# Softmax denominators summed by ScalarE over the maxima's tiles, and values multiplied as they leave their bank

## The reference

```python
q = x @ Wq.T + bq; k = x @ Wk.T + bk; v = x @ Wv.T + bv      # 16 query heads, 4 key heads, 32 wide
q = _apply_rope(q); k = _apply_rope(k)
att = jnp.einsum('bhgqd,bhkd->bhgqk', q, k) / scale
att = jnp.where(causal, att, jnp.asarray(-jnp.inf, att.dtype))
att = jax.nn.softmax(att, axis=-1)
y = jnp.einsum('bhgqk,bhkd->bhgqd', att, v)
return y @ Wo.T + bo
```

## Time and profile before

| | |
|---|---|
| median of 3 runs | 2018.44 us (2017.76 to 2019.21) |
| the profiled execution | 2016.81 us, span 2015.1 us |
| TensorE / VectorE / ScalarE / GpSimd busy | 83% / 44% / 28% / 23% of the span |
| granted TensorE clock, mean | 0.888 of full |
| start until the first score exponential | 110.3 us |
| the attention's last values copied out (L1066) | 1067.9 us |

### The profile page before, as it was taken

How to read it: one execution, slowest core, us unless ns; L and a number is a source line. 1 busy time by engine, 2 the same in 40 slices (tenths; PEclk the granted TensorE clock), 3 DMA queues, 4 the chain that set the end, 5 groups by cost and what they waited for, 6 DMA issues and landing times.

```text
span 2015.1 us, 23148 instructions
## 1 busy us (share of the span) xinstructions
PE 1669.5 (83%) x7518; PEld 1002.2 (50%) x7519; DVE 882.4 (44%) x1986; ACT 570.8 (28%) x1083; POOL 467.3 (23%) x653
## 2 busy tenths in 40 slices
PE   4488888888888888888865599999799999999940
PEld 4254554555545555455433487888444444444420
DVE  2444547456464564645634453222222222222239
ACT  2133324234342343423442211111122222222213
POOL 0111222122221222212211112222122222222237
PEclk8678888888898888988976799999899999999975
DMA  3344354254542545415332336775457664665468
GB/s 121 47 78 75 79 126 106 73 130 92 126 111 74 126 95 126 116 43 126 80 136 73 152 130 223 244 260 177 154 135 239 163 190 103 162 163 129 74 183 348
DMA packets 117598, 271.53 MB, mean 135 GB/s; under 512 B 15364, under 2 KB 40966, under 8 KB 110600
## 3 DMA queue, kind: packets, MB, share of 16 engines
q1 hardware_dynamic: 100984, 232.42, 39.9%
q0 software_dynamic: 16496, 37.63, 9.5%
HBM read 248.62 MB, written 109.34 MB: 178 GB/s over the span
## 4 chain that ended last, share of the span: by engine, by line
PE 66%; DVE 11%; issue 8%; ACT 5%; DMA 4%; POOL 4%; SPq 1%; POOLq 0%; DVEq 0%; ACTq 0%
PE bank L1767 26%; PE bank L1968 11%; PE bank L1985 5%; PE bank L1871 4%; PE bank L1848 4%; PE bank L1874 3%; PE bank L1831 3%; DVE tmp L1230 2%; PE bank L1958 1%; PE bank L1972 1%; ACT P L1058 1%; DVE rp L1238 1%; PE bank L1833 1%; ACT xin L1016 1%; PE bank L1978 1%
## 5 line engine op out<-in xcount | busy, mean ns | idle before, releaser
L1298 DVE TENSOR_REDUCE mx<-bank 128x1 f32<-128x512 f32 (+3 forms) x352 | 219.3, 634 | 209.4 <-PE bank L1833 208.4
L1058 ACT ACTIVATE P<-bank 128x512 f32<-128x512 f32 x320 | 190.5, 595 | 411.2 <-PE bank L1848 410.4
L1968 PE MATMUL bank<-ring,xg 128*128 x632 | 285.1, 594 | 0.0
L1831 PE MATMUL bank<-Ks,Qs 96*128 96x384 f32 (+3 forms) x512 | 167.4, 394 | 68.3 <-DVE mx L1298 36.7
L1848 PE MATMUL bank<-Qs,Ks 97*128 97x512 f32 x320 | 162.1, 507 | 42.9 <-ACT P L1058 37.1
L1767 PE MATMUL bank<-xt,ws 128*128 128x512 f32 x768 | 182.9, 395 | 2.7 <-DMA xt<-xt_scratch 2.7
L1968 PEld LDWEIGHTS bank<-ring,xg 128*128 128x128 f32 x632 | 114.3, 191 | 114.6 <-issue 114.6
L1767 PEld LDWEIGHTS bank<-xt,ws 128*128 128x128 f32 x768 | 146.2, 190 | 35.7 <-DMA xt<-xt_scratch 3.6
L1674 POOL TENSOR_SCALAR_AFFINE_SELECT P<-P 128x256 f32<-128x256 f32 (+1 forms) x192 | 93.2, 488 | 301.8 <-ACT P L1058 301.7
L1831 PEld LDWEIGHTS bank<-Ks,Qs 96*128 96x128 f32 x512 | 107.9, 228 | 109.7 <-DVE mx L1298 51.8
L1767 PE MATMUL bank<-wo_s,ynr 128*128 128x512 f32 x384 | 132.0, 470 | 35.0 <-DVE x L1357 23.9
(11 more groups left out here) (227 smaller groups left out, 2396.9 us busy)
## 6 DMA issues: line engine op xcount, KB each, us to landing
ring<-in_w SPq DMA_DIRECT2D x79, 1024.0 KB
ring<-in_w SPq DMA_DIRECT2D x79, 512.0 KB
Qs<-st SPq DMA_DIRECT2D x192, 128.0 KB, 4.7
xs<-xs_scratch SPq DMA_DIRECT2D x79, 258.0 KB, 3.7
xs_scratch<-xs_scratch SPq DMA_DIRECT2D x78, 258.0 KB, 5.0
xt<-xt_scratch SPq DMA_DIRECT2D x32, 512.0 KB, 6.4
xs<-xn_scratch SPq DMA_DIRECT2D x64, 256.0 KB, 2.9
xt_scratch<-xt SPq DMA_DIRECT2D x30, 512.0 KB, 4.8
```

What stands on the lines that cost most here:

```text
L1058: e.activation(Pt[:, p, :], bank[PA.bank[step]][:, :], ACT.Exp, scale=SCALE).then_inc(s_exp, 1)
L1298: e.tensor_reduce(mx[:, G % 2, :].rearrange("p (h i) -> p h i", i=4)[:, h:h + n, i:i + 1], bank[PA.bank["max", b, p, j]][:, 0:n * k].rearr ...
L1831: e.matmul(ps[:, o * k:o * k + k], Qs[0:96, 4 * g + h + o, i * 128:(i + 1) * 128], Ks[0:96, b % 2, g, 0:k], start=o == 0, stop=False)
L1968: e.matmul(ps[:, :].rearrange("p (o n) -> p o n", o=1), xg[:, q, 128 * k:128 * k + 128], ring[:, bass.ds(reg[n], 1), 512 * k:512 * k + 512 ...
```

## The change

Denominators no longer come from TensorE. After VectorE has reduced a first-pass tile (now to minima, since the scores are formed with the opposite sign), ScalarE takes the exponential of the same tile in place, with the row's minimum as bias pointer and the sum along the row as a second output: one instruction for each head, 512 in all. VectorE takes reciprocals of 128x16; minima and reciprocals are turned together (32 columns for 16), both split in two, and go out in four DMAs: two rows (96 and 97) of Qs and two rows of a small tile rd. `rb` spreads the reciprocals with one product per quarter of a batch, before the last `pv` of it; ScalarE copies the spread ones to SBUF, VectorE multiplies the values as they leave their bank, and the product is split from there. The ones-matmuls, the denominators' bank and their chain at the end of a batch go. Maxima get the freed third bank, `maxT` moves to the general ones, and the rates change.

```diff
-    G, M, U, PS = Banks(0, 3), Banks(3, 2), Banks(5, 1), Banks(0, NP)
+    G, M, U, PS = Banks(0, 3), Banks(3, 3), Banks(6, 1), Banks(0, NP)
...
+        def tiles():
+            for n in range(NMAX + 2):
+                if n < NMAX:
+                    P.on(M, P.add("max", b, p, n))
+                if 1 <= n <= NMAX:
+                    P.add("mred", b, p, n - 1)
+                if n >= 2:
+                    P.add("mexp", b, p, n - 2)
+                    M.done(P.bank["max", b, p, n - 2])
                 yield
-            s = P.add("maxT", b, g)
-            P.on(M, s)
-            yield
-            P.add("mTcp", b, g)
-            M.done(P.bank[s])
-        for n in range(NMAX):
-            s = P.add("max", b, p, n)
-            P.on(M, s)
-            if n > 0:
-                M.done(P.bank["max", b, p, n - 1])
-            yield
-            if n == 5:
-                yield from wait(4)
-            if n == MAX_OF[0] + 1:
-                P.add("maxdo", b, p, n)
-                M.done(P.bank["max", b, p, n])
+                if n == 5:
+                    yield from wait(4)
+        def turns():
+            for j in range(2):
+                g = 2 * p + j
+                while ("mexp", b, p, MAX_OF[j] - 1) not in P.nth:
+                    yield
                 yield
-                yield from turn(2 * p)
-        P.add("maxdo", b, p, NMAX - 1)
-        M.done(P.bank["max", b, p, NMAX - 1])
-        yield
-        yield from turn(2 * p + 1)
-        yield
+                P.add("mrec", b, g)
+                yield
+                yield from claim("maxT", b, g)
+                yield
+                P.add("mThi", b, g)
+                yield
+                P.add("mTlo", b, g)
+                freed("maxT", b, g)
+                yield
+        yield from beside(tiles(), turns())
...
+                after.extend([("rbs", b, p, qh), ("ymul", b, p, qh), ("yhi", b, p, qh), ("ylo", b, p, qh)])
...
+                    if late[0] < qh:
+                        yield from claim("rb", b, p, late[0])
...
-        side = [(maxima(b, 1), 1.3)]
+        side = [(maxima(b, 1), 1.35)]
         if more:
-            side.append((chain(prep(b + 1), proj(b + 1, 0), move(b + 1, 0, 0)), 46 / H))
+            side.append((chain(prep(b + 1), proj(b + 1, 0), move(b + 1, 0, 0)), 2.0))
             nought = zeros(b)
             side.append((islice(nought, 6), 0.25))
         if tails is not None:
-            side.append((islice(tails, 34), 34 / H))
+            side.append((islice(tails, 24), 24 / H))
...
+            side.append((maxima(b + 1, 0), 1.35))
...
+            side.append((tails, 1.3))
...
+                    for n in range(2):
+                        e.dma_start(Qs[96 + n:97 + n, 4 * g:4 * g + 4, :].bitcast(F32), mT[0:16, G % 2, n, :].bitcast(F32)).then_inc(
+                            d_m[G % 2], 16)
+                    for n in range(2):
+                        r = 4 * n + 2 * (g % 2)
+                        e.dma_start(rd[r:r + 2, g // 2, :, :].bitcast(F32), mT[16:32, G % 2, n, :].bitcast(F32)).then_inc(d_m[G % 2], 16)
...
+                elif kind == "mexp":
+                    b, p, j = a
+                    g_, h, n, i = MAX_TILES[j]
+                    G, k = 4 * b + 2 * p + g_, 128 * (i + 1)
+                    ps = bank[PA.bank["max", b, p, j]]
+                    w.wait_ge(max_dve, PA.nth["mred", b, p, j])
+                    if G >= 2:
+                        w.wait_ge(l_dve, G - 1)
+                    for o in range(n):
+                        c = 4 * (h + o) + i
+                        m = e.activation(ps[:, o * k:o * k + k], ps[:, o * k:o * k + k], ACT.Exp, scale=-1.0, bias=mr[:, G % 2, 0, c:c + 1],
+                                         accum_out=se[:, G % 2, c:c + 1])
+                    m.then_inc(max_act, 1)
...
+                    e.activation(reciprocals_of(b, p, qh), bank[PA.bank["rb", b, p, qh]][:, :], ACT.Copy).then_inc(rbs_act, 1)
+                elif kind == "yhi":
+                    b, p, qh = a
+                    w.wait_ge(y_dve, PA.nth["ymul", b, p, qh])
+                    e.activation(values_of(b, qh)[:, 0, 2 * p:2 * p + 2, :],
+                                 bank[PA.bank["rb", b, p, qh]][:, :].rearrange("p (h q) -> p h q", h=2), ACT.Copy).then_inc(y_hi, 1)
...
+                elif kind == "mrec":
+                    b, g = a
+                    G = 4 * b + g
+                    w.wait_ge(max_act, PA.nth["mexp", b, g // 2, MAX_OF[g % 2] - 1])
+                    e.reciprocal(mr[:, G % 2, 1, :], se[:, G % 2, :]).then_inc(l_dve, 1)
...
+                    e.tensor_tensor(ps[:, :], bank[7][:, :], reciprocals_of(b, p, qh), ALU.mult).then_inc(y_dve, 1)
...
+                    e.tensor_tensor(y[:, 1, 2 * p:2 * p + 2, :], bank[PA.bank["rb", b, p, qh]][:, :].rearrange("p (h q) -> p h q", h=2),
+                                    y[:, 0, 2 * p:2 * p + 2, :], ALU.subtract).then_inc(y_lo, 1)
...
-                        e.matmul(queries(bank[6][32 * j:32 * j + 32, :], qh, kc), Vs[:, b % 2, kc, 2 * p + j // 2, :], rows[j],
-                                 start=kc == 0, stop=last)
-                    for j in range(4):
-                        m = e.matmul(queries(bank[7][32 * j:32 * j + 32, :], qh, kc), ov[:, n, :], rows[j],
-                                     start=kc == 0 and n == 0, stop=last and n == 3)
+                        m = e.matmul(queries(bank[7][32 * j:32 * j + 32, :], qh, kc), Vs[:, b % 2, kc, 2 * p + j // 2, :], rows[j],
+                                     start=kc == 0, stop=last)
...
-                        m = e.matmul(ps[:, :], sel_s[:, 2 * p + qh, :], rc[:, n, :], start=n == 0, stop=n == 1)
-                    m.then_inc(rb_pe, 1)
+                    e.matmul(bank[PA.bank[step]][:, :].rearrange("p (h q) -> p h q", h=2), sel_s[:, :], rd[:, p, :, 256 * qh:256 * qh + 256],
+                             start=True, stop=True).then_inc(rb_pe, 1)
```

More of the change, by code:

```diff
@@ L253, in values, with turn @@
             if kc == 2 * qh + 1:
-                P.add("yev", b, p, qh)
+                after.extend([("rbs", b, p, qh), ("ymul", b, p, qh), ("yhi", b, p, qh), ("ylo", b, p, qh)])
+        def turn():
+            if after:
+                s = P.add(*after.pop(0))
+                if s[0] == "ylo":
+                    freed("rb", *s[1:])
         for qh in range(2):
@@ L268, in heads @@
                 late = (qh, kc, slots)
+        yield from claim("rb", b, p, 1)
         values(*late)
-        yield
-    def values_ready(b, qh):
-        for p in range(3):
-            if p < 2:
-                yield from claim("rb", b, qh, p)
-            if p > 0:
-                P.add("ynm", b, qh, p - 1)
-                freed("rb", b, qh, p - 1)
-            yield
-            if p > 0:
-                P.add("ynhi", b, qh, p - 1)
-                yield
-                P.add("ynlo", b, qh, p - 1)
-                yield
+        while after:
+            yield
+            turn()
     def front(b, i):
@@ L339, in tail @@
             yield from beside(back(b, 0), front(b, 1))
-            yield from beside(back(b, 1), chain(values_ready(b, 1), front(b, 2)))
+            yield from beside(back(b, 1), front(b, 2))
             yield from beside(back(b, 2), front(b, 3))
@@ L352, in rest @@
     def rest():
-        for j in range(5):
+        for j in range(4):
             P.add("late", j)
@@ L1663, in _ @@
                     e.tensor_tensor(st[o, 2:4, :], rp[o, :, :], st[o, 0:2, :], ALU.subtract).then_inc(st_lo, 1)
-                elif kind == "late" and a[0] == 4:
+                elif kind == "late" and a[0] == 3:
                     e.memset(zero[:, :], 0.0).then_inc(pool_const, 1)
```

243 lines of the change are left out of this document (91 added, 152 removed).

## The result

The changed kernel takes 2313.45 us (median of 4, 2312.28 to 2316.18), the kernel before on the same chip 2018.15 (4 runs). The ratio is 1.146, 95% interval 1.144 to 1.148: 295 us slower. I had forecast slower by 37. Direction and stalls were right, the size was not.

The account below looks back on a forecast made before the run. PE was taken to bound the batch, busy 85%. Batches 1 to 6 +55, batch 0 -3, batch 7 -8, end -11, start +4: +37 on 2018.4 gave 2055 us, forecast range 2022 to 2095 (0.48), 8 in 10 between 1975 and 2125.

Parts of the forecast that it names:

- The wait for Q: Middle of batches 1 to 6: PE stands 17 us (14 to 20) at the first maxima tile for Q's DMA.
- ScalarE's price: New exponentials with sums cost ScalarE 17 us per half batch (14 to 20), the sums 2.9 of it, ceiling 5.7.
- stretch 1: First 16 scores of batch 3's first half: ACT, busy 33 us, ends it at 38 us for 50.3.
- PE's relief: Ones-matmuls and half the spreading go from PE's path: 11.3 us per batch, 90 in eight batches.
- The spreading matmul: L1885, from two products per half to one: 1.3 of 2.7 us per batch go, 1.2 expected to show.
- over 80%: Sign of a right forecast: ACT's busy share in stretch 1, at about 33 us.
- Stretches 2 and 3: First half's last four scores: 43 us (26 plus a 17 us stall) for 19.9; second half: 54.4 for 56.0.
- Batch 0: First batch, 101.7 us, without a stall: PE -11, ACT nearly as long as PE, so -3 us.
- Rival (c): Granted clock falls from 0.88 to 0.80 over the whole attention: 2115 us, chance 0.03.
- Rival (b): ACT saturates, output-tile steps wait behind exponentials and PE for them: about 2125 us, chance 0.12.
- The end: Behind the last batch, output products start earlier without the denominators' chain: -11 us.
- The start: Kernel start, where extra DMA issues and the first tiles' longer chain are not hidden: +4 us.

Follow-up runs that it names:

- run 3: Changed kernel, with the planner freeing a transposed input tile's bank before the next transpose claims one: 2163.3 us median, 2117 fastest.
- run 9: Kernel before, with the ones-matmuls kept only for the first block of keys of each group: 2003.2 us, ratio 0.993.
- run 4: Changed kernel with the bank freed first as in run 3 and all 512 new exponentials left out as in run 2: 1975.5 us, ratio 0.979.
- run 6: Changed kernel with 80 idle products on PE in each of the six waits for Q: 2288.5 us, ratio 1.134.
- run 12: Kernel before, with 512 exponentials and sums added on ScalarE whose results nobody uses: 2156.7 us, ratio 1.069.
- run 2: Changed kernel without the 512 new exponentials, a tile's bank free after VectorE's minimum: 2130.3 us, ratio 1.057.
- run 8: Kernel before, with each of the 320 score products done twice: 2054.5 us, ratio 1.017.
- run 15: run 3 with statistics and normalization of the input planned earlier, at the end of the batch ahead: 2119.8 us, ratio 1.050.
- run 1: Changed kernel without the sums along the row, denominators a constant: 2264.7 us, ratio 1.123.
- run 14: run 3 with two banks instead of three for the maxima, one score bank and one bank idle: 2503.5 us, ratio 1.242.

## Why the prediction was right and wrong

- **The wait for Q** held: 16.5 to 17.4 us six times, forecast 17 (14 to 20). K's products end at 666.16 and the tile starts at 695.00: 28.8 for 28.9. Without it (run 3) the time is 150 to 196 us less, not 103.
- **ScalarE's price** held: 17.1 us of L1059 in stretch 1 and 18.0 in stretch 3, forecast 17; stretch 1's total 32.75 for 33. The single terms were off both ways: exponentials cheaper (340 for 376, 665 for 691), the sum a separate instruction of 210 ns, over my ceiling of 179, of which 94 count.
- **PE's relief** of 11.3 us per batch was the first failed step: "all of it lies on PE's path". The work went (10.9 us at the old clock), but the time did not follow: run 9 gives a quarter of what it removes, run 4 42 of 101, since the clock falls with the work. The spreading matmul, too, took 644 ns (median) four times in batch 3, 2.6 us for the forecast 1.2.
- **Stretch 1** was the second: "So ACT, not PE, ends stretch 1 ... 38 us". ScalarE was busy 32.75 us as said, but the stretch took 53.6. Neither engine ended it: ScalarE was busy 61% of it, where "over 80%" was a sign of being right. PE waited 10.6 us for banks that ScalarE held, ScalarE 13.8 for PE's scores, and PE did its part at 0.63. I added the busy times of two in-order engines as if the longer hid the shorter. The 2 us for waits of tiles and 3 for the normalization were far too little: PE alone stood 17.0 us (53.60 less 36.64).
- **Stretches 2 and 3**: 37.5 and 65.7 for 26 and 54.4 (the wait apart), from the clock behind the stall, "costing 2 more", and the waits. V's products alone took 4.9 us more (11.0 for 6.1), at 413 ns for 277.
- **Batch 0** is the cleanest miss, as it has no wait for Q: +19 for -3. PE was busy 99.6 us for 86.3, at 0.67 for 0.83.
- **By size**, a batch overran its forecast of 135.4 us by 38.7. The clock was put at 2 and measured 28.8, which is 26.8 of it. The waits besides the one for Q were left 1.5 of the forecast's 9.2 and measured 13.1, which is 11.6. The relief and the wait for Q were right.
- **Rival (c)** named the mechanism, with 3% and a clock of 0.80; it was 0.68 over batches 0 to 6. I had reasoned that the clock only scales what is busy, from 0.88, and had nothing from which to say how far it goes down. Rival (b)'s waits came as well; its price, 2125, was for them alone.
- **The end** was better than forecast: the output products start 3.6 us after the last score exponential for 15.4, 11.8 us earlier (forecast 11), with PE busy up to them. A second such gap, 5.4 us ahead of the last half's output products (1102.24 to 1107.62 before), went as well, and I had not counted it; with products at a higher clock 21 us came back for 11. The batches bury it. The start cost 8.1 for 4.

The sum by what was measured: -11.3 relief, +17.3 wait for Q, +13.1 other waits, +28.8 clock are the 47.9 of a batch.

The Trainium skill (TensorE: Matmul & The Clock Gate, section HAM oscillation — how this bites in real kernels) says that work behind a long enough wait starts at half rate. This case's trace agrees: the clock was 0.50 over the first 3 us behind the wait of 17.31 us, and with the wait filled (run 6) it was 1.00 and the time 25 us less. I had quoted it in the prediction and put 2 us to it.

Open stays how the 0.43 (run 12) to 0.7 us (run 2) per us of ScalarE's load divide between its places of waiting. Moving the normalization only moved its wait, and the other places were not tried one by one, since no bank was left to decouple both maxima and scores. Open too is what sets the clock: runs 6 and 8 show that filling PE's time raises it and run 9 that emptying it lowers it, but run 3 has batches with the same instructions and the same idle time at two clocks.

## What to carry to other kernels

Before work is taken off TensorE and put on an engine that feeds it, read how the granted clock stands in the stretch: at 0.83 to 0.90 with holes in it, each new wait costs once as a wait and again as work at 1.2 GHz, and most of the relief is given back (42 us of 101 arrived in run 4, 15 of 57 in run 9). Two in-order engines that hold each other's banks don't hide one another; count the banks between them, and try the number of banks first (340 us between two and three here). To see what the clock costs, weigh PE's busy time with it: if that product is unchanged, the work is, and the rest is clock. A wait that is moved is not yet gone: sum the engine's idle time before and after (184 and 198 us for run 15). A planner that claims a bank before it frees one can starve a whole projection; freeing first is one moved step and was worth 150 to 196 us here.

## What the runs showed of the hardware

- The sum along the row is an instruction of its own (ACTIVATION_READ_ACCUMULATOR, 183 ns from SBUF in run 12, 210 from PSUM in the kernel after) that overlaps the next one: 94 ns net by run 1.
- An exponential of 512 from PSUM back to PSUM with a pointer for its bias takes 665 ns; from SBUF to SBUF on 64 partitions 717 (run 12).
- 480 products nobody reads made a kernel 25 us faster (run 6); in the kernel before, 320 score products done twice cost 36 us for 77.
- Batches with the same instructions and the same PE idle time (30.6 and 30.3 us) took 143.1 and 150.2 us in one execution, at a granted clock of 0.76 and 0.72 (run 3).
- With the same instructions in the same order on every engine, one PSUM bank less for the maxima made the kernel 340 us slower (386 against the fastest execution), at a clock of 0.73 to 0.74 for 0.81 to 0.84 (run 14 and run 3).
